# The first batch's loads are issued behind waits for earlier landings (SyncE, one core)

## The reference, cut to what matters

```python
h = einsum('bsh,bhk->bsk', x, W_down[role]) + b_down[role][:, None, :]   # H = 1024, K = 512
h = gelu(h)
u = einsum('bsk,bkh->bsh', h, W_up[role]) + b_up[role][:, None, :]
y = x + u
mean, var = mean(y), mean(square(y - mean(y)))                            # over the 1024 columns
out = (y - mean) * rsqrt(var + 1e-5) * gamma[role] + beta[role]
```

## Time and profile before

| | |
|---|---|
| median of 3 runs | 366.18 us (365.87 to 366.7) |
| the profiled execution | 365.91 us |
| its span, first to last instruction | 364.1 us |
| mean granted TensorE clock | 0.993 |
| PE busy | 353.2 us (97%) |
| DVE, ACT, POOL busy | 288.3, 185.4, 40.6 us |
| DMA | 96.59 MB, mean 265 GB/s |

### The profile page before, as it was taken

One profiled execution on the slowest core, in us unless ns is written; L12 is line 12 of the kernel. 1 busy time (PEld: TensorE's weight loads), 2 busy tenths in 40 slices (PEclk: granted clock), 3 DMA queues, 4 the chain that ended last, 5 costly groups with the idle time before them and its releaser, 6 DMA issues.

```text
span 364.1 us, 4944 instructions
## 1 busy us (share of the span) xinstructions
PE 353.2 (97%) x1548; PEld 289.4 (79%) x1548; DVE 288.3 (79%) x297; ACT 185.4 (51%) x295; POOL 40.6 (11%) x71
## 2 busy tenths in 40 slices
PE   6999999999999999999999999999999999999991
PEld 3788888878888888888888888888888888888881
DVE  2697989897896878968798787986789777873475
ACT  4684565762546626564375623656355571714131
POOL 0000221003200112002110021100310002200011
PEclk9999999999999999999999999999999999999997
DMA  7999999979878887779669696886977822580023
GB/s 205 398 401 412 410 403 387 325 278 367 323 248 288 237 340 259 262 264 325 255 220 364 225 361 227 258 277 227 376 263 221 305 93 78 214 282 3 0 115 116
DMA packets 27227, 96.59 MB, mean 265 GB/s; under 512 B 3154, under 2 KB 3410, under 8 KB 27218
## 3 DMA queue, kind: packets, MB, share of 16 engines
q1 hardware_dynamic: 23040, 81.80, 63.7%
q10 hardware_dynamic: 4178, 14.69, 10.2%
HBM read 79.70 MB, written 16.78 MB: 265 GB/s over the span
## 4 chain that ended last, share of the span: by engine, by line
PE 94%; DMA 2%; SPq 1%; DVE 1%; ACT 0%; issue 0%; POOLq 0%; DVEq 0%; POOL 0%; ACTq 0%
PE up_ps L270 48%; PE down_ps L263 46%; DMA wd_stage<-W_down 2%; DMA roles_sb<-roles 0%; DVE rows L570 0%; ACT wd_hi L344 0%; POOLq L42 0%; DVE rows L546 0%; SPq L147 0%; ACT squares L394 0%; SPq L171 0%; SPq L233 0%; SPq L234 0%; DVEq L42 0%; POOL var_eps L483 0%
## 5 line engine op out<-in xcount | busy, mean ns | idle before, releaser
L263 PE MATMUL down_ps<-x_hi,wd_hi 128*128 128x512 f32 x256 | 81.6, 390 | 2.2 <-ACT wd_hi L454 1.6
L263 PE MATMUL down_ps<-x_lo,wd_hi 128*128 128x512 f32 x256 | 81.4, 389 | 0.0
L263 PE MATMUL down_ps<-x_hi,wd_lo 128*128 128x512 f32 x256 | 81.4, 389 | 0.0
L270 PE MATMUL up_ps<-wu_hi,h_hi 128*128 128x512 f32 x256 | 79.6, 389 | 0.1
L270 PE MATMUL up_ps<-wu_hi,h_lo 128*128 128x512 f32 x256 | 79.5, 389 | 0.0
L270 PE MATMUL up_ps<-wu_lo,h_hi 128*128 128x512 f32 x256 | 79.4, 389 | 0.0
L263 PEld LDWEIGHTS down_ps<-x_hi,wd_hi 128*128 128x128 f32 x256 | 47.8, 188 | 13.1 <-issue 3.3
L270 PEld LDWEIGHTS up_ps<-wu_hi,h_hi 128*128 128x128 f32 x256 | 47.9, 188 | 10.5 <-issue 0.7
L263 PEld LDWEIGHTS down_ps<-x_lo,wd_hi 128*128 128x128 f32 x256 | 48.1, 188 | 10.0
L270 PEld LDWEIGHTS up_ps<-wu_lo,h_hi 128*128 128x128 f32 x256 | 48.1, 188 | 10.0
L270 PEld LDWEIGHTS up_ps<-wu_hi,h_lo 128*128 128x128 f32 x256 | 48.1, 188 | 10.0
(11 more groups left out here) (45 smaller groups left out, 253.0 us busy)
## 6 DMA issues: line engine op xcount, KB each, us to landing
wu_stage<-W_up SPq DMA_DIRECT2D x32, 512.0 KB, 6.7
rows<-x SPq DMA_DIRECT2D x32, 512.0 KB, 3.8
x_stage<-xT SPq DMA_DIRECT2D x31, 512.0 KB, 9.1
wd_stage<-W_down SPq DMA_DIRECT2D x31, 512.0 KB, 9.1
out<-rows ACTq DMA_DIRECT2D x28, 512.0 KB, 4.8
b_up_row<-b_up SPq DMA_DIRECT2D x8, 512.0 KB, 3.9
gamma_row<-gamma SPq DMA_DIRECT2D x8, 512.0 KB, 6.1
beta_row<-beta SPq DMA_DIRECT2D x8, 512.0 KB, 6.9
```

Of the source, the lines that this page charges most:

```text
L263: return pe.matmul(down_ps[:, kc, :], wd_part[:, n, c * K + kc * P:c * K + (kc + 1) * P], x_part[:, n, c * S:(c + 1) * S], start=start, st ...
L270: mm = pe.matmul(up_ps[:, t % 2, half], h_part[:, kc, t * P:(t + 1) * P], wu_part[:, kc, half], start=(kc == 0 and h_part is h_hi and wu_p ...
```

## The change

SP waits between the loads of the first batch. Before part 2 (x and W_down) it waits for the landing of W_down part 0, before part 3 for W_down part 1, before W_up part 0 for W_down part 2, and before W_up part 1 for W_down part 3 (the same wait stands before parts 2 and 3, where it is already met). Part 1 is not made to wait.

```diff
             sp.dma_start(wd_stage[:, 0, K:CPL * K], wd_src(first_role)[:, 0, K:CPL * K]).then_inc(wd_landed[0], 16)
+
             for i in range(1, NLOAD):
+                if i > 1:
+                    sp.wait_ge(wd_landed[i - 2], 16)
                 load_x_part(0, i)
                 load_wd_part(first_role, i)
             for i in range(KC):
+                sp.wait_ge(wd_landed[min(NLOAD - 2 + i, NLOAD - 1)], 16)
                 load_wu_part(first_role, i)
             load_ahead(1, load_role(sp, 1), 0)
```

## The result

The changed kernel takes 369.76 us (median of 6 runs, 369.45 to 370.31), the kernel before 365.89 (6 runs beside them): ratio 1.0089, 95% interval 1.0059 to 1.0119. It is slower by 3.3 to 3.9 us. The profiled execution took 370.17 us, its span is 368.4 us, 4.3 us longer than before. The same kernel, run again later beside other runs of before, gave 1.0095 (1.0077 to 1.0113); its profiled execution took 369.54 us with a span of 367.7.

The account below looks back on a forecast made before the run. PE bounds most of the span, but a chain without slack from the stream of loads reaches it up to 77.6 us; the 1.5 us shift is paid in full: 365.91 + 1.5 = 367.4 us, range 365.6 to 368.5.

Parts of the forecast that it names:

- The bound and the chain: PE bounds most of the span; up to 77.6 us a chain without slack from the stream of loads reaches it.
- Step (a): Waits ahead of x and W_down parts 2 and 3: price 0, at most 0.2 us; W_down part 3 lands 16.6 to 17.4.
- step (c): Wait ahead of W_up part 1, one part open: last engine 0.7 us late, at most 1.5; mean engine loses 2.1 us.
- Step (b): Wait ahead of W_up part 0 ends at 14.7 us, 2.5 us before the last engine finishes W_down part 3: price 0.
- The shift d: Delay of the landing at 36.71 us (second batch's W_down part 1): between 0.7 and 2.1 us, taken as 1.5.
- lag of the last engine, rebuilt: By the landing at 36.71 us an engine falls behind the mean anew, by half of the former lag of about 2 us.
- Rival D: W_up part 1 takes 3.9 us and the last engine's lag returns in full: 2.9 us, 368.8 us; chance 0.07.
- A: Rival: no engine falls behind anew, only the last engine's 0.7 us or less arrive: 366.2 to 366.7 us; chance 0.25.
- B: Rival: W_down part 1 lands before 11.4 us, stream behind it no later, PE's waits go: 365.0 us; chance 0.08.
- C: Rival: the change does nothing, as SP's issues were early enough that no engine empties: 365.9 to 366.2 us; chance 0.08.
- The rule of the Trainium skill: A DMA takes 2.0 us plus bytes over 436 GB/s; 0.8 us bare behind one open part, estimate about 366.7 us.
- PE's stop at 47 us: Sum of tile 1 ends at 46.9 us where PE wanted it at 46.00: a stall of 0.9 us.

Follow-up runs that it names:

- The second trace: The kernel before, run again with no edit: ratio 1.0024 (0.9996 to 1.0051), span 364.1 us.
- the fourth set: The kernel before with a single wait ahead of W_up part 1, moved to earlier landings: three parts open 366.48 us, two open 367.47 us.
- the single-wait kernel: The kernel before with one wait, for W_down part 3 ahead of W_up part 1: 368.76 us, ratio 1.0077.

## Why the prediction was wrong

The direction and the chain were right, the size was not: 367.4 us forecast, 369.8 measured, 1.3 us over the upper end of the range.

- **The bound and the chain**: right. I read from 0.3 us of a late matmul that the stream of loads sets the end with no slack. The second trace and the table above show it far more strongly than I put it: 0.9 us of PE's lead vanish.
- **Step (a), "price 0, at most 0.2"**: wrong, and the first step that failed. By the medians these waits alone cost 1.4 to 1.7 us (in their one trace the rows come 0.5 us late). In the changed kernel W_down part 3 landed at 17.9 us in both traces, past the 17.4 that I had as the worst case, and PE waited 0.57 and 0.28 us for it at 20.3 us: the sign of an underpriced step (a) that I had named. I asked only when that part lands for PE. I did not ask what engines that were already through with part 2 did meanwhile, though step (c) counts just that. The open work at that landing was two parts.
- **Step (b), price 0**: not tested by itself. In the changed kernel that wait ended at 15.4 us with x and W_down part 3 open, two parts, and in the first trace engines stood still around it (0.68 and 0.71, 15 to 17 us). A single wait with two parts open cost 1.2 us in the fourth set, so a price of 0 has no support.
- **Step (c), last engine 0.7 to 1.5 us, mean engine 2.1**: the mechanism held. By 18.45 us the changed kernel had moved 18.45 x 256 = 4.72 MB and the kernel before 18.45 x 303 = 5.59: 0.87 MB less, where the prediction had 0.86. From W_down part 3 to W_up part 1 it took 4.0 us in place of 2.56, so 1.5 us in the landing of the last engine, the upper end. In the single-wait kernel the landing at 36.7 us moved by 3.3 us by this step alone, more than the 2.1 that I took for the most that the mean engine could lose.
- **The shift d, "between 0.7 and 2.1"**: the term that was mis-sized most, 4.2 and 3.8 us in the two traces. The upper bound rested on two things: that no time is lost outside step (c), and that the stream runs at its full rate once it is full again. Neither held. The wait of step (c) ended 0.65 us later than I had it, so the gap lasted until 19.1 us and 1.09 MB were behind by then, 2.6 us of work; from 19.1 to 36.7 us the stream ran at 365 GB/s against 407 with the engines busy (share 1.01), another 0.74 MB or 1.8 us. The "lag of the last engine, rebuilt" was the wrong picture for the second part, since the whole stream is slower there, b_up most of all.
- **Rival D** had the right direction and was still 1 us short; A, B and C fell. The first half of B's condition came about in the first trace of the changed kernel, W_down part 1 at 10.8 us and PE's wait for it gone, and brought nothing. The waits did not bring that landing forward in any way that shows: it came at 10.4 to 12.05 us in the seven traces without waits ahead of parts 2 and 3, and at 10.2 to 11.5 in the seven with them, and by the second trace of the kernel before it would not have mattered.
- **The rule of the Trainium skill** (DMA: Bandwidth & Descriptors, Anatomy of one DMA: 2.0 us plus bytes over 436 GB/s): the page gives it for DMAs that GpSimd issues, and these are issued by SP; the prediction did not say so. For 512 KB it makes an estimate of 3.2 us, measured 3.9 behind the wait. By its 2.0 us two open parts would hide the fixed part; the runs show that two do not and three do. The measurement decides.
- **PE's stop at 47 us**: forecast 0.9 us, measured 2.1, in line with d, since both hang on it.

What stays open is why the transfers are slower for some 10 us behind a gap, and with it why d is near 4 us and not near the 2.6 us of the gap. That the engines come into step and then ask for the same places at once would fit the slow broadcast, but it was only argued. A wait for the first engine's landing and not the last's was not tried, since it can pass part-way through a load.

## What to carry to other kernels

Where a stream of loads runs without a hole and a chain without slack hangs on it, price every wait ahead of an issue by the work that stays open when it ends: here three parts of 512 KB (3.8 us) were free, two cost 1.2 us and one 2.9 by the medians, against 3.1 to 3.9 us from issue to landing. Count lost bytes over all engines and follow them to the end of the full stream, not only the landing that is awaited next, and don't take it that the stream is at once at full rate. A tiny gap of PE at the end of another engine's gapless run can be the sign of the true bound: a second trace of the same kernel, in which something early came out otherwise, shows it for nothing.

## What the runs showed of the hardware that I had not expected

- Behind a gap the stream is slower with busy engines: 371 GB/s from 20 to 36.7 us against 406, and 325 against 401 from 24 to 30 us.
- A load of one 4 KB row to 128 partitions lands 1.2 to 1.6 us behind the part before it in the kernel before, and 2.2 to 2.4 us in the changed kernel's two traces, behind a gap; the plain load of the same size there 1.27.
- PE's granted clock fell to 0.52, the level of 1.2 GHz, behind a stop of 2.05 us in one execution of the changed kernel and stayed at 1.00, the level of 2.4 GHz, behind one of 2.10 us in another.
